# Attention with 16 heads: maxima taken in units of 512 scores, one unit in eight through ScalarE and a difference of keys, and four banks for the scores

## The chip, the cores and the metric

The kernel runs on one core of a Trainium2 chip. The metric is device time in microseconds (us) of the whole program, lower is better. PE is TensorE, DVE is VectorE, ACT is ScalarE, POOL is GpSimd and SP is SyncE.

## The reference

Four layers follow each other on x of shape (2, 2048, 256): an attention over 44 fixed offsets, eight grouped feed-forward products, a full attention with rotary positions, and the feed-forward products again. The change touches the third:

```
q, k, v = qkv[:, :, 0], qkv[:, :, 1], qkv[:, :, 2]        # 16 heads of 16
q = q * cos + rotate_half(q) * sin
k = k * cos + rotate_half(k) * sin
scores = jnp.einsum('bqhd,bkhd->bhqk', q, k) * DH ** -0.5
attn = jax.nn.softmax(scores, axis=-1)                    # over all 2048 keys
out = jnp.einsum('bhqk,bkhd->bqhd', attn, v).reshape(b, l, d)
return out @ Wo
```

The softmax subtracts the maximum over the 2048 keys of each query.

## The kernel before

The program has three stages with a barrier between them. The **local stage** works through eight chunks of 512 tokens: the first attention, the folded feed-forward weights, and at a chunk's end the rotated queries and keys of the full attention, split in two fp16 parts (`qparts`) and written to HBM (`q_d`, `k_d`). What each engine does next there is set by lists of positions (`DVE_STEPS`, `ACT_STEPS` and so on): each step has a place inside a chunk's slots, and `order_of` sorts them. The step `rotate` makes rotated values in `rope_q` (i of 0 and 1 are queries, 2 and 3 keys), ACT casts them to the high half, `rest` makes the low half on DVE, and `last` stores both.

The **attention stage** has 32 iterations (two batches, four groups of four heads, four chunks of 512 queries). An iteration y handles 16 key tiles of 128 keys. For each key tile PE computes four score matmuls, one per head, `ps_s[128 keys, 512 queries]`, ACT takes the exponential of each bank (L1422) into `pr`, and PE multiplies `pr` by the values into `ps_o` two key tiles later (`weigh`, L1353, two parts of 256 queries; each fp32 matmul shows as two). Scores are in fp16, with their contraction of 50 rows in one half of the PE array, so that two scores (heads of even and odd index) can run beside each other. Two of the 50 rows carry the negative maximum of each query, so that the exponential needs no other bias.

These maxima are computed one iteration ahead, beside the scores. For each pair of heads, each tile of 128 queries and each quarter of 512 keys, `max_unit` issues two matmuls of 48 rows (one head in each half of the array, L1311) into `ps_m[:, u % 2]`, two banks of 512 each, and DVE reduces 1024 numbers to two maxima (L1433). That is 32 units per iteration and two per key tile. After the last unit of an iteration's maxima, DVE makes the negative maxima in three small steps (L309, L311, L312), put between its next units. PE transposes them into a score bank (`max_rows`, L1318), DVE copies them out (L1447), and SP writes them into the rows of `qs` by DMA.

PE's order of work is written out in `iteration`: per key tile a max unit, two scores, the first part of `weigh`, a max unit, two scores, the second part. So a key tile has two like halves, and PE starts a half by waiting for a max bank. Scores rotate through `SB` = 3 banks: score n needs that the exponential of n-3 is done (`bank_free`). Max units rotate through two double banks. At `OUTPUT_AT` (n = 6) of the next iteration ACT copies the finished `ps_o` (L1413), which PE waits for ahead of that iteration's first `weigh`.

PSUM has eight banks: three for scores, four for maxima, one for the output.

Of the kernel before, what the change touches and what calls it, by code (L numbers as in the profile page):

```python
# [77 lines left out]
for _m, (_c, _bank, _r, _g) in enumerate(PRODUCTS):  # L78
# [64 lines left out]
    (68.079, "last", 3)]  # L143
# [17 lines left out]
    (66.977, "rest", 2), (71.781, "rest", 3)]  # L161
# [158 lines left out]
def local_stage(nc, I, D, A):  # L320

    with ExitStack() as ctx:  # L322
# [28 lines left out]
        qparts = sb("qparts", [P, 2, PARTS, CH], F16)  # L351
        nrm = sb("nrm", [P, 2], F32)
# [45 lines left out]
        def ahead_place(u):  # L398
# [21 lines left out]
            sem(n) for n in ("qkb_ps", "qkb_read", "rope_sum", "rope_high", "qparts_ready"))  # L420
        nrm_sb, nrm_ps, bound_sb, factor_step, scaled = (
# [11 lines left out]
        def parts(j, i):  # L433
            return (qparts_last if j == NG - 1 and i >= 2 else qparts)[:, i % 2]

# [12 lines left out]
        def _(sp):  # L448
# [101 lines left out]
            for s in range(2):  # L550
                sp.wait_ge(qparts_stored[s], 32 * NG)
            sp.wait_ge(nmt_stored, 64)
# [258 lines left out]
        def _(act):  # L811
# [17 lines left out]
            def step(j, what, i):  # L829
# [65 lines left out]
                elif what == "rotate":  # L895
                    act.wait_ge(rope_sum, j * 4 + i + 1)
                    act.copy(parts(j, i)[:, 0, :], rope_q[:, i % 2, :]).then_inc(rope_high, 1)
# [18 lines left out]
        def _(dve):  # L916
# [13 lines left out]
            def step(j, what, i):  # L930
# [111 lines left out]
                elif what == "rotate":  # L1042
# [12 lines left out]
                    dve.tensor_tensor(rope_q[:, i % 2, :], rope_a[:, :], rope_b[:, :],  # L1055
                                      ALU.add if i % 2 else ALU.subtract).then_inc(rope_sum, 1)
                elif what == "rest":
                    dve.wait_ge(rope_high, j * 4 + i + 1)
                    dve.tensor_tensor(parts(j, i)[:, 1, :], rope_q[:, i % 2, :], parts(j, i)[:, 0, :],
                                      ALU.subtract).then_inc(qparts_ready, 1)  # L1060

# [101 lines left out]
def full_attention(nc, I, D, A, F):  # L1163
# [4 lines left out]
    MAXU = MAXIMA * NCH  # L1168
# [4 lines left out]
    ROWS_KT = KT - AHEAD + 2  # L1173
    ROWS_AT = GRP * ROWS_KT + 2
    SCORES = KT * GRP
    OPS = SCORES + 1
    SB = 3
# [3 lines left out]
    QK_LOADS = 16 * 6 * (1 + NCH)  # L1181
    NEG = 16 * 2

    with ExitStack() as ctx:
# [4 lines left out]
        ps_m = ctx.enter_context(nc.psum_tensor("ps_m", [P, 2, 2, CH], F32))  # L1189
        ps_o = ctx.enter_context(nc.psum_tensor("ps_o", [P, CH], F32))  # L1190
        vg = sb("vg", [P, KT, GRP, SLOT], F32)
        pr = sb("pr", [P, PR_RING, GRP, CH], F32)
        q0_ld = sem("c_q0_ld")
        (qk_ld, qk_ready, va_ld, vb_ld, vc_ld, s_ps, p_ready, pv_done, m_ps, m_read, nm_step,
         nmt_ps, nmt_sb, neg_ld) = (sem("c_" + n) for n in (
             "qk_ld", "qk_ready", "va_ld", "vb_ld", "vc_ld", "s_ps", "p_ready", "pv_done", "m_ps",
             "m_read", "nm_step", "nmt_ps", "nmt_sb", "neg_ld"))
# [3 lines left out]
        def unit_place(u):  # L1201

            return u // (TILES * NCH), u // NCH % TILES, u % NCH
# [15 lines left out]
        def _(sp):  # L1219
            for n in range(2, NCH):  # L1220
# [82 lines left out]
        def _(pe):  # L1303
            def max_unit(u, taken, q, slot):

                if taken - FIRST >= 2:
                    pe.wait_ge(m_read, taken - FIRST - 1)
# [422 lines left out]
```

## Time and profile before

| | us |
|---|---|
| median of 3 runs | 2123.95 (2120.16 to 2124.56) |
| the profiled execution | 2122.61 |
| its span, first to last instruction | 2120.8 |
| local stage, up to the barrier | about 832 |
| attention stage | about 832 to 2011 |
| last stage | about 2011 to 2120.8 |

Over the span PE is busy 2011.0 us, DVE 1838.1, ACT 1523.0 and POOL 764.6. Times of one instruction (mean ns) include its tail: the next instruction of the same engine starts before it ends, so the pace of an engine is read from start to start. PE's ends are modelled. The granted clock of PE is 0.964 of full speed over the span, and full between 1000 and 1900 us.

### The profile page before, as it was taken

The page shows a single profiled execution, that of the slowest core. Times are in us where ns is not written, and L with a number is a line of the kernel's source. Part 1 is how long each engine was busy: PE and PEld are TensorE (multiplying, and loading weights), DVE is VectorE, ACT ScalarE, POOL GpSimd, SP SyncE. Part 2 cuts the span into 40 slices and gives each one's busy share as a digit, 9 for nine tenths or more (in the row PEclk, how much of TensorE's full clock was granted, in tenths as well). Part 3 has the DMA queues.
Part 4 walks back from the last instruction along what each step waited for, and adds up shares of the span by engine and source line. Part 5 has one row for each costly group of instructions (what it writes and reads, how often), then busy time and mean ns, then how long its engine had stood idle before and what let it go on. Part 6 is the DMA issues. An engine that isn't in the chain of part 4 may idle for free. (4 is left out here: it accounts for less than half of the span.)

```text
span 2120.8 us, 46870 instructions
## 1 busy us (share of the span) xinstructions
PE 2011.0 (95%) x18498; PEld 798.8 (38%) x18498; DVE 1838.1 (87%) x2195; ACT 1523.0 (72%) x3579; POOL 764.6 (36%) x1019
## 2 busy tenths in 40 slices
PE   7889999999998886999999999999999999999978
PEld 5444455555553432333333333333333333333333
DVE  3697888898886775999999999999999999999255
ACT  0155676666663413999999999999999999999911
POOL 2499899999998203603003003002000000052100
PEclk9999999999999757999999999999999999999989
DMA  8365565566567414302002001001000000031321
GB/s 279 125 140 124 127 153 136 143 158 157 127 149 161 114 34 102 81 7 55 5 7 54 7 15 46 4 25 36 5 27 5 7 24 7 9 121 58 98 71 53
DMA packets 228811, 161.86 MB, mean 76 GB/s; under 512 B 152809, under 2 KB 199865, under 8 KB 228585
## 3 DMA queue, kind: packets, MB, share of 16 engines
q1 hardware_dynamic: 198272, 112.61, 21.5%
q0 software_dynamic: 14944, 31.33, 5.5%
q10 hardware_dynamic: 15376, 14.93, 2.1%
q8 instruction: 147, 2.41, 0.5%
q14 instruction: 72, 0.58, 0.1%
HBM read 97.64 MB, written 44.11 MB: 67 GB/s over the span
## 5 line engine op out<-in xcount | busy, mean ns | idle before, releaser
L1422 ACT ACTIVATE pr<-ps_s 128x512 f32<-128x512 f32 x2048 | 1087.1, 596 | 72.7 <-PE ps_s L1335 25.9
L1433 DVE TENSOR_REDUCE mx<-ps_m 128x2 f32<-128x1024 f32 x980 | 1124.3, 1213 | 10.6 <-PE ps_m L1311 8.9
L1353 PE MATMUL ps_o<-pr,vg 128*32 128x256 f32 x8192 | 654.8, 392 | 8.1 <-ACT f_ou L1413 8.1
L588 POOL TENSOR_TENSOR room<-qs 128x512 f32<-128x512 f32 x336 | 414.8, 1268 | 79.7 <-ACT qs L855 54.4
L1335 PE MATMUL ps_s<-qs,ks 50*128 50x512 f16 x2048 | 423.2, 382 | 0.5 <-ACT pr L1422 0.5
L1311 PE MATMUL ps_m<-ks,qs 48*128 48x512 f16 x1960 | 384.5, 388 | 9.4 <-PEq L322 9.4
L1267 POOL DMA_DIRECT2D vg<-vb_d x24 | 19.6, 819 | 976.3 <-PE ps_o L1353 893.9
L1353 PEld LDWEIGHTS ps_o<-pr,vg 128*32 128x32 f32 x8192 | 162.6, 108 | 273.6 <-issue 245.6
L1311 PEld LDWEIGHTS ps_m<-ks,qs 48*128 48x128 f16 x1960 | 93.9, 92 | 413.0 <-issue 278.1
L927 DVE TENSOR_TENSOR room<-PSa,qs 128x512 f32<-128x512 f32 x368 | 234.1, 678 | 14.1 <-PE PSa L681 13.6
L1335 PEld LDWEIGHTS ps_s<-qs,ks 50*128 50x128 f16 x2048 | 188.8, 94 | 119.9 <-ACT pr L1422 38.6
L681 PE MATMUL PSa<-room,sj 128*32 128x512 f32 x1408 | 197.9, 608 | 9.1 <-POOL room L588 4.4
L878 ACT ACTIVATE attn<-PSa,red 128x44 f32<-128x44 f32 x416 | 117.0, 312 | 9.3 <-DVE red L1009 4.5
L878 ACT ACTIVATION_READ_ACCUMULATOR attn<-PSa,red 128x1 f32 x416 | 92.6, 223 | 0.0
L885 ACT COPY room<-PSa 128x512 f32<-128x512 f32 x128 | 69.2, 595 | 31.8 <-PE PSa L753 31.3
L1260 POOL DMA_DIRECT2D qs<-q_d x168 | 83.6, 504 | 1.1 <-issue 1.1
L644 PE MATMUL PSa<-tail_room 128*128 128x256 f32 x256 | 64.7, 410 | 13.7 <-DMA tail_room<-in_W2T 9.2
L890 ACT COPY oT<-PSa 128x128 f32<-128x128 f32 x64 | 17.9, 280 | 80.9 <-PE PSa L768 80.8
L603 POOL TENSOR_TENSOR far<-far,fart 128x128 f32<-128x128 f32 x128 | 69.2, 541 | 10.0
L753 PE MATMUL PSa<-ident,room 128*128 128x128 f32 x512 | 72.5, 287 | 0.3 <-DMA room<-skew 0.3
L753 PEld LDWEIGHTS PSa<-ident,room 128*128 128x128 f32 x512 | 59.9, 147 | 31.6 <-issue 28.4
L957 DVE TENSOR_REDUCE mx<-PSa 128x1 f32<-128x512 f32 x88 | 54.9, 683 | 16.3 <-PE PSa L665 16.3
(162 smaller groups left out, 1906.9 us busy)
## 6 DMA issues: line engine op xcount, KB each, us to landing
room<-skew SPq DMA_DIRECT2D x128, 208.0 KB, 4.0
skew<-attn SPq DMA_DIRECT2D x64, 164.0 KB, 4.2
tail_room<-in_W SPq DMA_DIRECT2D x32, 256.0 KB, 3.4
tail_room<-in_W2T SPq DMA_DIRECT2D x32, 256.0 KB, 4.1
vb_d<-vb SPq DMA_DIRECT2D x8, 1024.0 KB, 6.0
qs<-ks SPq DMA_DIRECT2D x26, 256.0 KB, 5.7
ks<-k_d POOLq DMA_DIRECT2D x48, 128.0 KB, 3.2
qs<-q_d POOLq DMA_DIRECT2D x180, 32.0 KB, 2.9
```

The lines of the kernel that those rows point to most:

```text
L588: pool.tensor_tensor(prod_p[:, n % RING, :], qT[:, c, :], kT[:, c, col:col + CH], ALU.mult).then_inc(prod_p_ready, 1)
L603: pool.tensor_tensor(total, total, part, ALU.add).then_inc(far_step, 1)
L681: pe.matmul(PS[SLOT * g:SLOT * (g + 1), SC_BANK, :], sj[:, BANK_J * bank + 4 * g + r, :], rhs[:, n % RING, :], start=(r == 0), stop=(r == ...
L753: tr = pe.transpose(PS[:, TURN_BANK[half], h * P:(h + 1) * P], own[:, w % 2, 4 * half + h, :], ident[:, :])
L878: ex = act.activation(attn[:, w % 2, h, :], logits[:, h, :], ACT.Exp, bias=red[:, w % 2, 0, h:h + 1], accum_out=red[:, w % 2, 1, h:h + 1])
L927: dve.tensor_tensor(prod_d[:, n % RING, :], PS[:, Q_BANK[c], :], kT[:, c, col:col + CH], ALU.mult).then_inc(prod_d_ready, 1)
L1260: pool.dma_start(qs[rows, g * NCH + n, :, :], D["q_d"][Q_STACK[i], :, heads, b * T + (1 + n) * CH:b * T + (2 + n) * CH]).then_inc(qk_ld, 16)
L1311: mm = pe.matmul(ps_m[:, u % 2, t, :], qs[rows, q, pair, tile * P:(tile + 1) * P], ks[rows, slot, pair, quarter * CH:(quarter + 1) * CH], ...
L1335: pe.matmul(ps_s[:, op % SB, :], ks[rows, slot, j // 2, kt * P:(kt + 1) * P], qs[rows, q, j // 2, :], start=True, stop=True).then_inc(s_ps, 1)
L1353: mm = pe.matmul(ps_o[SLOT * j:SLOT * (j + 1), cols], vg[:, kt, j, :], pr[:, kt % PR_RING, j, cols], start=(kt == 0 and part == 0), stop=( ...
L1422: act.activation(pr[:, kt % PR_RING, j, :], ps_s[:, place_of(y, n) % SB, :], ACT.Exp, scale=exp_scale).then_inc(p_ready, 1)
L1433: dve.tensor_reduce(mx[:, x % MX_RING, :, pair * TILES + tile, quarter], ps_m[:, u % 2, :, :], AX_X, ALU.max).then_inc(m_read, 1)
```

## The change

A max unit is now one matmul of 512 scores in one bank (two units where there was one, 64 per iteration), and `ps_m` has three banks. The freed bank goes to the scores (`SB` = 4). PE's order puts the four units of a key tile singly between the scores and the parts of `weigh`.

Of each eight units in a row, unit 1 (`is_less`) multiplies the queries by a difference of keys, the first quarter minus the second, for the odd head of a pair: ACT takes relu of it into `over` in SBUF. Unit 5 (`is_both`) is the same query tile and head with the second quarter: DVE adds `over` to it and takes the maximum, since max(a, b) = relu(a - b) + b. So DVE handles seven units of eight. The place in `mx` of the quarter left out is set to the lowest fp32 number once.

The differences are made in the local stage, twice (once per batch, in its second chunk): the rotated keys of a batch's first chunk stay in `first_k`, DVE subtracts (`diff`), ACT casts, DVE makes the low half (`diff_rest`), ACT stores to `kd_d` (`diff_last`). The attention stage loads them into `kd` beside the keys.

```diff
-    MAXU = MAXIMA * NCH
+    MAXU = 2 * MAXIMA * NCH
+    CYCLE, LESS, BOTH = 2 * NCH, 1, 5
+    QUARTERS = (0, 2, 1, 3)
+    START = FIRST + CYCLE
+    M_BANKS = 3
-    SB = 3
+    SB = 4
-    QK_LOADS = 16 * 6 * (1 + NCH)
+    QK_LOADS = 16 * (6 * (1 + NCH) + 3)
...
+            def max_unit(n, q, slot):
+                old = n - M_BANKS
+                if old >= FIRST:
+                    if is_less(old):
+                        pe.wait_ge(m_over, overs(old + 1))
+                    else:
+                        pe.wait_ge(m_read, reads(old + 1))
+                t, pair, tile, quarter = unit_place(n)
+                rows = half(t, 0, KROWS)
+                keys = kd[rows, slot, pair, :] if is_less(n) else ks[rows, slot, pair, quarter * CH:(quarter + 1) * CH]
+                pe.matmul(ps_m[:, n % M_BANKS, :], qs[rows, q, pair, tile * P:(tile + 1) * P], keys,
+                          start=True, stop=True).then_inc(m_ps, 1)
...
+                    if x == 1 and kt == (START - FIRST) // PER_TILE:
+                        pe.wait_ge(kd_ld, 16 * len(K_STACK))
+                    score(x, GRP * kt, q, slot)
                     tile_max(x, PER_TILE * kt)
-                    score(x, GRP * kt, q, slot)
                     score(x, GRP * kt + 1, q, slot)
...
                     tile_max(x, PER_TILE * kt + 1)
                     score(x, GRP * kt + 2, q, slot)
                     score(x, GRP * kt + 3, q, slot)
+                    tile_max(x, PER_TILE * kt + 2)
                     if older >= 0:
                         weigh(older // KT, older % KT, 1)
+                    tile_max(x, PER_TILE * kt + 3)
...
+            def take_less(n):
+                k = overs(n)
+                if k >= 2:
+                    dve_unit = n - 2 * CYCLE + BOTH - LESS
+                    act.wait_ge(m_read, reads(dve_unit + 1))
+                act.wait_ge(m_ps, n - FIRST + 1)
+                act.activation(over[:, k % 2, :], ps_m[:, n % M_BANKS, :], ACT.Relu).then_inc(m_over, 1)
...
+                        unit = (y + 1) * MAXU + CARRY + n - 1
+                        if is_less(unit) and unit < ITERS * MAXU:
+                            take_less(unit)
                         act.wait_ge(s_ps, y * SCORES + n + 1)
...
+                if is_both(n):
+                    dve.wait_ge(m_over, overs(n))
+                    above = over[:, (overs(n) - 1) % 2, :]
+                    dve.tensor_tensor_reduce(out=above, in0=ps_m[:, n % M_BANKS, :], in1=above, scale=1.0, scalar=LOWEST,
+                                             op0=ALU.add, op1=ALU.max, accum_out=best).then_inc(m_read, 1)
+                else:
+                    dve.tensor_reduce(best, ps_m[:, n % M_BANKS, :], AX_X, ALU.max).then_inc(m_read, 1)
...
+                elif what == "diff" and j % NCH == 1:
+                    dve.wait_ge(qparts_ready, j * 4 + i + 1)
+                    dve.tensor_tensor(rope_q[:, i % 2, :], first_k[:, i % 2, :], rope_q[:, i % 2, :],
+                                      ALU.subtract).then_inc(diff_ready, 1)
```

The order on PE in the attention stage, before. L1311 is a matmul for the maxima, L1335 a score, L1353 a part of `weigh`; the rows cover one key tile and a half.

```order
L1311 MATMUL ps_m<-ks,qs 128x512 x2
L1335 MATMUL ps_s<-qs,ks 128x512 x2
L1353 MATMUL ps_o<-pr,vg 32x256 x4
L1311 MATMUL ps_m<-ks,qs 128x512 x2
L1335 MATMUL ps_s<-qs,ks 128x512 x2
L1353 MATMUL ps_o<-pr,vg 32x256 x4
```

The same engine and stage now, one key tile (the first of two, the one with the difference `kd`): L1373 is a max unit, L1396 a score, L1414 a part of `weigh`.

```order
L1396 MATMUL ps_s<-qs,ks 128x512
L1373 MATMUL ps_m<-ks,qs 128x512
L1396 MATMUL ps_s<-qs,ks 128x512
L1414 MATMUL ps_o<-pr,vg 32x256 x4
L1373 MATMUL ps_m<-kd,qs 128x512
L1396 MATMUL ps_s<-qs,ks 128x512 x2
L1373 MATMUL ps_m<-ks,qs 128x512
L1414 MATMUL ps_o<-pr,vg 32x256 x4
L1373 MATMUL ps_m<-ks,qs 128x512
```

The two matmuls that stood together are apart: one comes between two scores or after two scores, the other directly behind a part of `weigh`.

DVE in the attention stage, at the place where an iteration's maxima end, before (with what each waits for):

```order
L309 TENSOR_REDUCE nm<-mx 128x16 [waits c_m_read]
L1433 TENSOR_REDUCE mx<-ps_m 128x2 [waits c_m_ps]
L311 TENSOR_SCALAR nmp<-nm 128x2x8 [waits c_nm_step,c_m_read]
L1433 TENSOR_REDUCE mx<-ps_m 128x2 [waits c_m_ps]
L312 SCALAR_TENSOR_TENSOR nmp<-nm,nmp 128x2x8 [waits c_nm_step,c_m_read]
```

The same place now. The two rows L1512 are one `tensor_tensor_reduce`: the add and maximum, and an instruction that writes the one result.

```order
L309 TENSOR_REDUCE nm<-mx 128x16 [waits c_mx_low,c_m_read]
L1515 TENSOR_REDUCE mx<-ps_m 128x1 [waits c_m_ps]
L311 TENSOR_SCALAR nmp<-nm 128x2x8 [waits c_nm_step,c_mx_low,c_m_read]
L1515 TENSOR_REDUCE mx<-ps_m 128x1 [waits c_m_ps] x2
L312 SCALAR_TENSOR_TENSOR nmp<-nm,nmp 128x2x8 [waits c_nm_step,c_mx_low,c_m_read]
L1512 ISA over,mx<-ps_m,over 128x512 [waits c_m_over,c_m_ps]
L1512 ISA mx 128x1
L1515 TENSOR_REDUCE mx<-ps_m 128x1 [waits c_m_ps] x3
```

The three small steps keep their spacing in scores, two units of 512 for one of 1024, and every eighth unit is missing from DVE's list.

On ACT the stage has one more instruction for eight exponentials (L1498):

```order
L1486 ACTIVATE over<-ps_m 128x512
L1498 ACTIVATE pr<-ps_s 128x512 x8
L1486 ACTIVATE over<-ps_m 128x512
L1498 ACTIVATE pr<-ps_s 128x512 x8
L1486 ACTIVATE over<-ps_m 128x512
```

Before, nothing but exponentials and one copy per iteration stood there.

## Rows read from the trace of the kernel before

**Rows 1.** Windows: stretch, PE, PEld, DVE, ACT, POOL busy (instructions), PEclk, DMA, GB/s

```profile
227.00:304.00 77.00, 76.98 (x695) 39.62 (x694) 67.43 (x101) 50.00 (x185) 70.35 (x81) 1.00 0.62 147
1000.00:1900.00 900.00, 892.92 (x9409) 282.12 (x9408) 898.71 (x883) 843.17 (x1589) 90.18 (x162) 1.00 0.09 24
```

**Rows 2.** Groups of instructions, 1000 to 1900 us: DVE

```profile
L1433 DVE TENSOR_REDUCE mx<-ps_m 128x2 f32<-128x1024 f32 x783 | 898.2, 1213 | 1.3
```

**Rows 3.** Timeline, PE alone: start us, us, instructions

```profile
1215.97 0.39 PE L1311 MATMUL ps_m<-ks,qs 48*128 48x512 f16 x2
1216.19 0.41 PE L1335 MATMUL ps_s<-qs,ks 50*128 50x512 f16 x2
1216.53 0.64 PE L1353 MATMUL ps_o<-pr,vg 128*32 128x256 f32 x8
1217.11 0.39 PE L1311 MATMUL ps_m<-ks,qs 48*128 48x512 f16 x2
1217.33 0.38 PE L1335 MATMUL ps_s<-qs,ks 50*128 50x512 f16 x2
...
1218.21 0.39 PE L1311 MATMUL ps_m<-ks,qs 48*128 48x512 f16 x2
...
1226.09 0.39 PE L1311 MATMUL ps_m<-ks,qs 48*128 48x512 f16 x2
```

**Rows 4.** Waits, 1000 to 1900 us: us in total, times, longest

```profile
PEld ps_m L1311 <- DVE mx L1433: 110.8, 269, 0.4
```

**Rows 5.** Timeline, DVE alone

```profile
1227.78 0.21 DVE L309 TENSOR_REDUCE nm<-mx 128x16 f32<-128x64 f32 x1
1227.90 1.22 DVE L1433 TENSOR_REDUCE mx<-ps_m 128x2 f32<-128x1024 f32 x1
1229.03 0.17 DVE L311 TENSOR_SCALAR nmp<-nm 128x16 f16<-128x16 f32 x1
1229.10 1.22 DVE L1433 TENSOR_REDUCE mx<-ps_m 128x2 f32<-128x1024 f32 x1
```

**Rows 6.** Timeline, ACT alone, in four short stretches

```profile
1207.85 0.58 ACT L1413 COPY f_ou<-ps_o 128x512 f32<-128x512 f32 x1
...
1244.69 0.58 ACT L1413 COPY f_ou<-ps_o 128x512 f32<-128x512 f32 x1
...
1980.99 1.09 ACT L1422 ACTIVATE pr<-ps_s 128x512 f32<-128x512 f32 x2
...
1981.94 0.63 ACT L1422 ACTIVATE pr<-ps_s 128x512 f32<-128x512 f32 x1
```

**Rows 7.** Timeline, PE and one of DVE, around the output copy and the transposed maxima

```profile
1207.71 0.39 PE L1311 MATMUL ps_m<-ks,qs 48*128 48x512 f16 x2
...
1209.15 0.39 PE L1311 MATMUL ps_m<-ks,qs 48*128 48x512 f16 x2
...
1209.58 1.23 DVE L1433 TENSOR_REDUCE mx<-ps_m 128x2 f32<-128x1024 f32 x1
...
1230.59 0.39 PE L1311 MATMUL ps_m<-ks,qs 48*128 48x512 f16 x2
...
1231.96 0.39 PE L1311 MATMUL ps_m<-ks,qs 48*128 48x512 f16 x2
```

**Rows 8.** Timeline of the local stage: units of 512 with three banks; two-input operations

```profile
783.26 2.48 DVE L957 TENSOR_REDUCE mx<-PSa 128x1 f32<-128x512 f32 x4 [0.46 <-PE PSa L665]
785.80 0.10 PEld L665 LDWEIGHTS PSa<-ks,qs 48*128 48x128 f16 x1 [0.50 <-DVE mx L957]
...
223.52 1.41 DVE L1039 SCALAR_TENSOR_TENSOR tail_room<-PSa,bcc,tail_room 128x512 f32<-128x512 f32 x2 [1.55 <-PE PSa L686]
```

**Rows 9.** The same operations by tile and line: duration ns min/median/max

```profile
L957 DVE TENSOR_REDUCE mx<-PSa x88: 629/681/693, 704.1 to 804.5; 128x1 f32<-128x512 f32 x88
L1039 DVE SCALAR_TENSOR_TENSOR tail_room<-PSa,bcc,tail_room x16: 741/748/752, 223.5 to 797.8; 128x512 f32<-128x512 f32 x16
```

**Rows 10.** Timeline, PE alone, last iteration, which computes no maxima

```profile
1996.74 0.48 PE L1335 MATMUL ps_s<-qs,ks 50*128 50x512 f16 x2
...
1998.77 0.48 PE L1335 MATMUL ps_s<-qs,ks 50*128 50x512 f16 x2
```

More of the change, by code:

```diff
@@ L434, in parts, with rotated @@
             return (qparts_last if j == NG - 1 and i >= 2 else qparts)[:, i % 2]
+        def rotated(j, i):
+            return (first_k if j % NCH == 0 and i >= 2 else rope_q)[:, i % 2, :]
         def qk_banks(j, i):
@@ L1219, in _ @@
         def _(sp):
+            load_differences(sp, 0, kd_ld)
             for n in range(2, NCH):
@@ L1303, in _ @@
         def _(pe):
-            def max_unit(u, taken, q, slot):
-                if taken - FIRST >= 2:
-                    pe.wait_ge(m_read, taken - FIRST - 1)
-                pair, tile, quarter = unit_place(u)
-                for t in range(2):
-                    rows = half(t, 0, KROWS)
-                    mm = pe.matmul(ps_m[:, u % 2, t, :], qs[rows, q, pair, tile * P:(tile + 1) * P],
-                                   ks[rows, slot, pair, quarter * CH:(quarter + 1) * CH], start=True, stop=True)
-                mm.then_inc(m_ps, 1)
+            def max_unit(n, q, slot):
[10 more added lines that the diff above has]
+                          start=True, stop=True).then_inc(m_ps, 1)
             def max_rows(x, bank):
@@ L1447, in max_rows @@
                 dve.tensor_copy(nmt[:, :], ps_s[0:PARTS * 16, bank, 0:P // 2].bitcast(F16)).then_inc(nmt_sb, 1)
+            plain = (START - MAXU) // CYCLE
+            for ring, first in ((0, 0), (1, plain), (2, 0)):
+                lower(ring, first, MAXIMA)
             for x in range(1, ITERS):
                 for e in range(MAXU):
-                    u = CARRY + e
-                    if x + u // MAXU < ITERS:
-                        max_unit(x + u // MAXU, u % MAXU)
-                    if 0 <= u - MAXU < NM_STEPS:
-                        max_parts(x, u - MAXU)
+                    n = x * MAXU + CARRY + e
+                    if n < ITERS * MAXU and not is_less(n):
+                        max_unit(n)
+                    part = (CARRY + e - MAXU) // 2
+                    if CARRY + e >= MAXU and e % 2 == 0 and part < NM_STEPS:
+                        max_parts(x, part)
+                        if x == 1 and part == NM_STEPS - 1:
+                            lower(1, 0, plain)
                     if e == PER_TILE * ROWS_KT:
```

78 lines of the change are left out of this document (58 added, 20 removed).

## The prediction

> **What bounds the kernel now.** I read the windows by stage first, then the groups of the attention stage, then short stretches of the timeline on one engine at a time. In the attention stage three engines look full: of 900 us PE is busy 893, DVE 899, ACT 843 [rows 1]. DVE's group explains its share at once: 783 reductions of 1024 scores with 1.3 us of idle time [rows 2], one start every 1.13 us (1227.90 to 1229.03, [rows 5]). One iteration takes 36.84 us (output copy to output copy, 1207.85 to 1244.69, [rows 6]; it repeats 29 times to the hundredth). DVE's own sum is 32 x 1.131 = 36.2, and the small steps add about 0.4 to 0.6.
>
> But DVE is not alone at that level. PE's timeline shows its own period: eight half key tiles from 1217.11 to 1226.09 are 8.98 us, so 2.246 us per key tile, and 16 x 2.246 = 35.94 [rows 3]. Two places per iteration are longer. The half that holds the wait for the output copy takes 1.44 instead of 1.11, and the half with the transposed maxima 1.37 instead of 1.11 [rows 7], so +0.33 and +0.27. The rest, 36.84 - 35.94 - 0.60 = 0.30, comes in the half behind each, where scores wait for one of three banks. So the PE sum is 36.84, and DVE, which falls back a little in each half, catches up at those two places. The wait list puts 110.8 us of PE's weight loads down to DVE, but in 269 pieces of 0.4 us, the length of the idle time between two groups of loads in any half [rows 4]: it is not lost time. A change that relieves DVE alone can't give back its whole relief; PE's pace of 2.246 is close behind.
>
> Inside a half the pieces are: 0.22 from the max pair to the score pair, 0.31 to 0.34 to `weigh`, 0.57 to the next max pair [rows 3]. The long halves are 0.03 longer than the short ones: there the second score starts late (the pair lasts 0.41 against 0.38), because it waits for the exponential three scores back. Short half: (2.246 - 0.03) / 2 = 1.109.
>
> **PE after the change.** The matmul count is the same. The order puts unit u7 and score s0 beside each other (opposite halves of the array), then u0 and s1, then `weigh`; then u1 and s2, s3 and u2, `weigh`, u3. So every unit still finds a partner, and I cost the reordering at nothing. With four score banks the 0.03 goes and so does the 0.30 behind the two long places. PE alone: 32 x 1.109 = 35.49, + 0.33 + 0.27 = 36.09 per iteration. That is the floor.
>
> **ACT.** When it has work, exponentials start every 0.477 us (1980.99 to 1981.94 are two, [rows 6]); one of the three there also waits for a second semaphore and costs nothing extra. 64 exponentials, 8 relus and the copy are 73 x 0.477 = 34.8 per iteration, 96% of the floor. In a cycle of two key tiles ACT is behind for four exponentials after a relu and just caught up at the end of the cycle. I count 0, with cover of 1.3 us per iteration; without it, ACT's wait would show as scores late by the difference.
>
> **DVE.** A reduction of 512 starts 0.60 us after the last (four from 783.26 end at 785.74; less 0.68 for the last, over 3, [rows 8, 9]); read more finely 0.598. Seven of eight units: per cycle of two key tiles 6 x 0.598 plus the fused one. I write the fused one as 0.598 + x. The trace does not show it. It is two instructions. From below: no faster than a reduction of the same length, and its second instruction like the smallest DVE steps, 0.07 from start to start (1229.03 to 1229.10, [rows 5]): x = 0.07. From above: the first instruction like the two-input one of L1039, which reads PSUM and SBUF and is followed by its like after 1.41 - 0.75 = 0.66 to 0.67 [rows 8, 9], the second 0.17, L311's whole duration [rows 5], because it has to wait for the first to end: x = 0.07 + 0.17 = 0.24. Between them, the nearest row (L1039 and then a small step) says 0.14, the plain reduction and a small step 0.07; I take x = 0.12.
>
> The Vector Engine (DVE) Microarchitecture Reference of the Trainium skill (section 7, Points that are easy to get wrong) says that this family of two-input instructions runs at half throughput when both sources are fp32 in SBUF. Here one source is PSUM, and the row of L1039 with one PSUM source shows full throughput, so I leave it to a rival.
>
> DVE's load is then 8 x (7 x 0.598 + x) + 0.4 + 0.1 = 34.9 per iteration, below PE. **But three single banks are a tighter ring than two double ones.** Before, two units of 1.13 us stood in the ring; now three of 0.6. Follow the ring in one cycle: DVE sits idle after u1 is left out, and starts u3 0.43 us after its matmul (1209.15 to 1209.58, [rows 7]). Then it runs u3, u4, u5, u6, u7 without a gap: u7 starts 4 x 0.598 + x = 2.39 + x later and ends 0.68 after that [rows 9]. PE's load of weights for u2 of the next cycle follows that end by 0.05 (785.80 behind 785.74, [rows 8]), and PE reaches its u3 0.88 us later (s3 and u2 together, 0.31 to `weigh`, 0.57 to u3). The ring closes with 0.43 + 2.39 + x + 0.68 + 0.05 + 0.88 = 4.44 + x. PE alone needs 4 x 1.109 = 4.436. So a cycle takes 4.44 + x: **each hundredth of x is paid eight times per iteration**, though DVE is idle 0.25 us per cycle. Queued behind the waiting load of u2 are `weigh` part 1, u3 and the next scores, so it is PE's time in full.
>
> Two of the eight cycles are those with the 0.33 and 0.27, which fall ahead of u2 and cover x there. The small step L312 now stands in the ring's gapless run (after u4): +0.08. L309, L311 and the copy of the rows fall in the idle 0.25. Iteration after: 36.09 + 0.08 + 6x = 36.17 + 6x. Against 36.84 the point of no gain is x = 0.11. With x = 0.12: 36.89, +0.05.
>
> **The sum.** 29 full iterations x 0.05 = +1.5. The last iteration and the end of the one before have no maxima: they take 2.03 us per key tile (1996.74 to 1998.77, [rows 10]) through three banks; with four they can go at ACT's 4 x 0.477 = 1.91, 0.12 x 20 key tiles = -2.4. Local stage: per batch 4 DVE instructions of 0.6, 2 casts and 2 DMA issues on ACT's queue, ahead of the next chunk's copies. PE is full there (76.98 of 77) and DVE is not (67.4) [rows 1], so 4.8 us of DVE work hide mostly; I take +1, at most +5. At the attention's start SP issues three loads of differences ahead of the query loads, and PE wants them in the third key tile: 0 to +1, counted in the 1. Sum: +0.1. The profiled execution took 2122.6 against a median of 2124.0 (+1.3), so I predict 2124 us.
>
> **Rivals.**
> A. The ring is not tight: PE's load for u2 finds its bank free, because the fused operation hides its second instruction or u7 starts earlier than I count. Then 36.17 to 36.6 per iteration, -0.67 to -0.24: 29 times that, less 1.4, is -21 to -8, 2103 to 2116. For it: DVE's load is 5% under PE's, and x near its lower bound gives the same (0.07: 36.59). Against: the ring closes within a hundredth of PE's own period, so nothing is spare.
> B. Slower: the fused operation is the one late thing, its place is the bank that u2 needs, and it decides from x = 0.13 on. With x = 0.24: 37.61, +0.77 x 29 = +22, less 1.4: 2145. For it: a result that is read out of the engine after the last element can hardly overlap the pass that makes it. Against: the small steps between reductions do overlap, 0.07.
> C. ACT becomes the bound: if relus and exponentials with two waits cost 0.1 each instead of nothing (24 per iteration), ACT needs 34.8 + 2.4 = 37.2, +0.4 x 29, so 2134. The two-wait exponential in [rows 6] speaks against it.
> D. The fused operation streams at half rate: x = 0.6, iteration 39.8, +3 x 29 = +85, 2210. By the skill's rule only where both sources are in SBUF.
>
> **How the numbers follow.** The forecast (x of 0.08 to 0.16, own range 2117 to 2131) has 0.48, A 0.23, B 0.22, C 0.04, D 0.03. A measurement can tell about 0.2% (4.2 us) from no change. Of the forecast's 0.48 about 0.13 fall below 2119.7, 0.27 within and 0.08 above 2128.2. Faster 0.13 + 0.23 = 0.36, same 0.27 + 0.03 from the near end of B = 0.30, slower 0.08 + 0.19 + 0.04 + 0.03 = 0.34. The range that holds 8 in 10 reaches into A and B: 2105 to 2142.
>
> **What would show it.** In the trace after: output copies 36.9 us apart (36.2: A; 37.3 and more: B or C). PE's long halves 1.14 gone. DVE idle about 0.25 us once per cycle, ahead of u3, and nowhere else; from the start of the fused instruction to that of the next reduction 0.72. PE's load for u2 waiting for DVE by about x, in six of eight cycles. ACT idle over 1 us per iteration. The last iteration at 1.91 per key tile. Wrong would be the whole line of thought if PE waited for DVE at other units than u2, if PE's half without waits were longer than 1.11 in the new order (a unit without a partner), or if ACT had no idle time.

## The result and the profile after

| | before | changed kernel |
|---|---|---|
| median of 20 runs each | 2124.26 us (2114.76 to 2137.77) | 2115.64 us (2108.85 to 2123.59) |
| ratio | | 0.9964, 95% interval 0.9948 to 0.9981 |
| span of the profiled execution | 2120.8 | 2112.9 |
| first matmul for the maxima in the attention stage, called its start below | 831.9 | 846.9 |
| from there to the last output copy | 1178.9 | 1156.8 |
| last stage | 110.0 | 109.2 |

The change made the kernel faster by 0.36%, 8 us. The prediction said no change, 2124 us. (On another chip the ratio was 0.9986 and its interval held 1, experiment 10.) The small difference is a sum of two large ones: in these two executions the attention stage gained 22.1 us, and the local stage ahead of it, where the differences of the keys are made, lost 15.1. (The changed kernel puts a score 0.4 us ahead of its first maximum, so counted from the stage's first matmul they are 21.7 and 14.7.) How firm the 15.1 is, a table behind the experiments tells. One execution below, the profiled one of the kernel with both moves, ran 1.5% long at a lower granted clock (0.918 against 0.965 to 0.968) and is left out of its ratio.

**The attention stage.** The windows view of the same stretch as in [rows 1] (PE, PEld, DVE, ACT, POOL busy, then PEclk, DMA and GB/s):

```profile
1000.00:1900.00 900.00, 893.55 (x9581) 265.64 (x9585) 865.84 (x1693) 896.33 (x1818) 107.23 (x195) 1.00 0.10 26
```

DVE fell from 899 to 866 and ACT rose from 843 to 896. PE's busy time hardly changed, but it got more instructions into the stretch. The groups of that stretch (busy us, mean ns of one, then the idle time before them), against [rows 2]:

```profile
L1498 ACT ACTIVATE pr<-ps_s 128x512 f32<-128x512 f32 x1594 | 812.6, 668 | 0.0
L1515 DVE TENSOR_REDUCE mx<-ps_m 128x1 f32<-128x512 f32 x1195 | 756.8, 683 | 34.2 <-PE ps_m L1373 30.9
L1512 DVE CUSTOM_DVE_ANT_0 over<-ps_m,over 128x512 f32<-128x512 f32 x199 | 135.6, 681 | 0.0
L1486 ACT ACTIVATE over<-ps_m 128x512 f32<-128x512 f32 x199 | 126.7, 637 | 3.7 <-DVE mx L1515 0.4
L1512 DVE DVE_READ_ACCUMULATOR2_ANT mx<- 128x1 f32 x199 | 16.5, 83 | 0.0
```

DVE has 34.2 us of idle time ahead of its plain reductions, where it had 1.3. The fused operation lasts as long as a plain reduction (681 against 683 ns). Its second instruction lasts 83 ns. What that one costs, only the order of starts tells. The timeline of DVE, one cycle of two key tiles (start, duration):

```profile
1206.86 0.68 DVE L1512 CUSTOM_DVE_ANT_0 over<-ps_m,over 128x512 f32<-128x512 f32 x1
1207.47 0.08 DVE L1512 DVE_READ_ACCUMULATOR2_ANT mx<- 128x1 f32 x1
1207.47 2.48 DVE L1515 TENSOR_REDUCE mx<-ps_m 128x1 f32<-128x512 f32 x4
1210.12 1.29 DVE L1515 TENSOR_REDUCE mx<-ps_m 128x1 f32<-128x512 f32 x2 [0.17 <-PE ps_m L1373]
1211.33 0.68 DVE L1512 CUSTOM_DVE_ANT_0 over<-ps_m,over 128x512 f32<-128x512 f32 x1
```

The next reduction starts 0.61 us after the fused operation, at the same 1207.47 as the read of the accumulator. Read more finely it is 0.606, so x = 0.606 - 0.598 = 0.008. The only idle time of the cycle is the one ahead of u3 (1210.12), as forecast. PE's timeline, the unit that reads the difference `kd` (u1), in two cycles:

```profile
1204.12 0.39 PE L1373 MATMUL ps_m<-kd,qs 48*128 48x512 f16 x1
...
1205.23 0.39 PE L1373 MATMUL ps_m<-ks,qs 48*128 48x512 f16 x1
...
1208.56 0.39 PE L1373 MATMUL ps_m<-kd,qs 48*128 48x512 f16 x1
...
1209.69 0.39 PE L1373 MATMUL ps_m<-ks,qs 48*128 48x512 f16 x1
...
1213.02 0.39 PE L1373 MATMUL ps_m<-kd,qs 48*128 48x512 f16 x1
```

The first cycle is 4.44 us, PE's own pace of 4 x 1.109; it is one of the two that follow a longer place. The second is 4.46: its first half, which holds u1 and u2, takes 1.13 (1208.56 to 1209.69) instead of 1.11. There PE's load of weights for u2 comes 0.05 behind the end of u7, whose bank it needs (timelines of DVE and PEld):

```profile
1208.07 0.68 DVE L1515 TENSOR_REDUCE mx<-ps_m 128x1 f32<-128x512 f32 x1
...
1208.80 0.09 PEld L1373 LDWEIGHTS ps_m<-ks,qs 48*128 48x128 f16 x1
```

So the ring of three banks is closed in the changed kernel. Read more finely, the 32 halves of one iteration are 24 of 1.109, six of 1.138 (those with u1 and u2 in six of the eight cycles), one of 1.436 with the wait for the output copy and one of 1.295 with the transposed maxima. A cycle that holds one of the six and no longer place takes 4.465. The copies of the output, which end an iteration, on ACT's timeline, with the relu beside the exponentials:

```profile
1204.61 0.60 ACT L1486 ACTIVATE over<-ps_m 128x512 f32<-128x512 f32 x1
1205.10 4.02 ACT L1498 ACTIVATE pr<-ps_s 128x512 f32<-128x512 f32 x8
1209.04 0.60 ACT L1486 ACTIVATE over<-ps_m 128x512 f32<-128x512 f32 x1
...
1216.51 0.59 ACT L1478 COPY f_ou<-ps_o 128x512 f32<-128x512 f32 x1
...
1252.68 0.59 ACT L1478 COPY f_ou<-ps_o 128x512 f32<-128x512 f32 x1
```

1252.68 - 1216.51 = 36.17, where [rows 6] had 36.84. (22 of the 29 full iterations take 36.17, the others 36.22 to 36.39.) The copies at the end lie at 1940.16, 1973.81 and 2003.75: 33.66 and 29.94 for the two iterations with few or no maxima (35.38 and 30.76 before).

**The local stage.** The stretch of [rows 1] from 227 to 304 is as before; the next chunk but one, the first that makes differences, is not (same columns):

```profile
227.00:304.00 77.00, 76.96 (x698) 39.62 (x694) 67.36 (x102) 50.45 (x184) 70.35 (x82) 1.00 0.64 148
321.00:412.00 91.00, 83.50 (x708) 42.69 (x708) 72.85 (x109) 53.24 (x190) 74.24 (x85) 0.94 0.54 126
```

The second row is the whole third chunk: the stores of x that end the chunks lie at 321.2 and 411.6, 90.4 us apart (77.0 before). PE stands for 7.5 us in two pieces. The first, on DVE's and PE's timelines (in brackets the idle time and who ended it):

```profile
366.80 3.25 DVE L1081 TENSOR_TENSOR tail_room<-first_k,tail_room 128x512 f32<-128x512 f32 x2
...
372.06 0.94 DVE L288 RECIPROCAL t_rs<-t_sd 128x128 f32<-128x128 f32 x1
```

```profile
373.05 1.55 PE L293 MATMUL PSa<-t_rs,spread 128*128 128x128 f32 x8 [2.51 <-DVE t_rs L288]
...
389.29 1.19 PE L264 MATMUL PSa<-t_xm,ones 128*128 128x512 f32 x1 [4.99 <-DVE t_xm L260]
```

The two new subtractions (L1081, step `diff`) took 3.25 us ahead of an inverse that PE waits for. The second piece is the wait of `diff_rest` (L1085) for ACT's cast:

```profile
385.58 1.05 DVE L1085 TENSOR_TENSOR first_k<-tail_room,first_k 128x512 f16<-128x512 f32 x1 [6.89 <-ACT first_k L909]
386.55 1.40 DVE L1055 SCALAR_TENSOR_TENSOR tail_room<-PSa,bcc,tail_room 128x512 f32<-128x512 f32 x2
387.87 0.68 DVE L1085 TENSOR_TENSOR first_k<-tail_room,first_k 128x512 f16<-128x512 f32 x1
388.47 0.68 DVE L260 TENSOR_TENSOR t_xm<-tail_room 128x512 f32<-128x512 f32 x1
```

DVE stood 6.89 us with the update of the residual (L1055) and the norm's input (L260) queued behind, and PE waits for the latter. The granted clock (PEclk, the third number from the end) fell to half twice, as the windows show:

```profile
373.00:377.00 4.00, 3.95 (x27) 2.37 (x31) 2.36 (x4) 0.00 (x0) 2.60 (x3) 0.58 1.05 307
377.00:387.00 10.00, 7.30 (x70) 3.34 (x62) 3.11 (x6) 6.56 (x24) 9.08 (x11) 1.00 0.47 125
387.00:394.00 7.00, 4.71 (x14) 1.57 (x15) 4.57 (x7) 0.60 (x2) 1.27 (x2) 0.52 0.00 0
```

A mean of 0.58 over 4 us is half clock for 3.4 us, 0.52 over 7 us for 6.7. The first of these stretches lies behind the first idle piece. The second lasts from 387.3 to 394.1 by the trace's records of the clock: it begins 2 us before the second piece ends (389.29) and reaches almost 5 us beyond it.

### The profile page after: what moved, and what is told of

Its sections match the earlier page's. It is cut to its first block and busy times, and to the rows that moved or that the text cites. A ratio compares the mean times of both kernels' runs of the same rounds, so it can differ in the third digit from the quotient of the medians.

```text
span 2112.9 us, 48657 instructions
## 1 busy us (share of the span) xinstructions
PE 1989.9 (94%) x18498; PEld 770.3 (36%) x18498; DVE 1792.2 (85%) x3187; ACT 1570.7 (74%) x3827; POOL 777.9 (37%) x1040
## 5 line engine op out<-in xcount | busy, mean ns | idle before, releaser
L1498 ACT ACTIVATE pr<-ps_s 128x512 f32<-128x512 f32 x2048 | 1042.8, 676 | 1.7 <-PE ps_s L1396 1.6
L1515 DVE TENSOR_REDUCE mx<-ps_m 128x1 f32<-128x512 f32 x1472 | 932.1, 684 | 45.3 <-PE ps_m L1373 41.5
L1414 PE MATMUL ps_o<-pr,vg 128*32 128x256 f32 x8192 | 655.0, 392 | 9.3 <-ACT f_ou L1478 8.6
L1396 PE MATMUL ps_s<-qs,ks 50*128 50x512 f16 x2048 | 612.4, 384 | 9.4 <-PEq L322 9.3
L1373 PE MATMUL ps_m<-ks,qs 48*128 48x512 f16 x1716 | 544.6, 384 | 0.0
L1414 PEld LDWEIGHTS ps_o<-pr,vg 128*32 128x32 f32 x8192 | 162.5, 108 | 333.8 <-issue 210.0
L1373 PEld LDWEIGHTS ps_m<-ks,qs 48*128 48x128 f16 x1716 | 142.3, 93 | 353.3 <-issue 203.7
L1512 DVE CUSTOM_DVE_ANT_0 over<-ps_m,over 128x512 f32<-128x512 f32 x244 | 166.2, 681 | 0.7 <-PE ps_m L1373 0.7
L1486 ACT ACTIVATE over<-ps_m 128x512 f32<-128x512 f32 x244 | 155.1, 636 | 5.5 <-PE ps_m L1373 1.3
L1396 PEld LDWEIGHTS ps_s<-qs,ks 50*128 50x128 f16 x2048 | 141.8, 93 | 29.5 <-ACT pr L1498 19.0
L1373 PE MATMUL ps_m<-kd,qs 48*128 48x512 f16 x244 | 94.5, 387 | 0.0
L879 ACT ACTIVATE room<-PSa,pbias 128x512 f32<-128x512 f32 (+1 forms) x48 | 33.1, 689 | 56.4 <-PE PSa L690 56.4
```

The lines of the kernel that those rows point to most:

```text
L1373: pe.matmul(ps_m[:, n % M_BANKS, :], qs[rows, q, pair, tile * P:(tile + 1) * P], keys, start=True, stop=True).then_inc(m_ps, 1)
L1396: pe.matmul(ps_s[:, op % SB, :], ks[rows, slot, j // 2, kt * P:(kt + 1) * P], qs[rows, q, j // 2, :], start=True, stop=True).then_inc(s_ps, 1)
L1414: mm = pe.matmul(ps_o[SLOT * j:SLOT * (j + 1), cols], vg[:, kt, j, :], pr[:, kt % PR_RING, j, cols], start=(kt == 0 and part == 0), stop=( ...
L1486: act.activation(over[:, k % 2, :], ps_m[:, n % M_BANKS, :], ACT.Relu).then_inc(m_over, 1)
L1498: act.activation(pr[:, kt % PR_RING, j, :], ps_s[:, place_of(y, n) % SB, :], ACT.Exp, scale=exp_scale).then_inc(p_ready, 1)
L1512: dve.tensor_tensor_reduce(out=above, in0=ps_m[:, n % M_BANKS, :], in1=above, scale=1.0, scalar=LOWEST, op0=ALU.add, op1=ALU.max, accum_ou ...
```

## The experiments

There are 12 runs: ten altered kernels, and the changed kernel and that of experiment 1 once more. Ratios are against the kernel before on the same chip. Runs without a ratio are a single execution each, and of them the iterations count. Iterations are read from the copies of the output. Of each edit the main lines are shown.

**1. `diff_rest` later.** The low halves on DVE, and with them its wait for ACT's cast, are moved behind the steps that PE needs, and so are the stores (`diff_last`). The casts stay where they were.

```diff
-(74.8, "diff_rest", 2), (75, "diff_rest", 3)]        # DVE_STEPS
+(82, "diff_rest", 2), (82.1, "diff_rest", 3)]
-(76.8, "diff_last", 2), (77.2, "diff_last", 3)]      # ACT_STEPS
+(85, "diff_last", 2), (85.2, "diff_last", 3)]
```

> The changed kernel with the low half of the key differences (diff_rest on DVE) moved from slot 75 to slot 82 of the chunk, and its store on ACT from 77 to 85; the attention stage is as it was. Theory: the local stage of the changed kernel is 15 us longer than before (barrier at 847 instead of 832) mainly because DVE stood 6.9 us at diff_rest until ACT had cast the difference, with the chunk's next norm behind it. Then this kernel has no such wait, its attention stage starts at 835 to 840, iterations stay at 36.17, and the time is 7 to 12 us below the changed kernel: ratio to before 0.991 to 0.993. Rival: the longer local stage comes from the added work itself or from scatter between executions, not from that wait: attention starts at 844 or later, ratio 0.996.

Measured: 2106.09 us, ratio 0.9940 (0.9923 to 0.9957). That is short of the expected ratio of 0.991 to 0.993. Attention starts at 835.5 instead of 846.9, the iteration is 36.17, and no wait at L1085 is left. The 11 us between the two starts are not all the wait's: the start of one and the same local stage scatters by more than that (table below). By the time it is 0.9964 - 0.9940, about 5 us, by the third and fourth chunk together about 6. The first piece stands:

```profile
370.62 1.16 PE L293 MATMUL PSa<-t_rs,spread 128*128 128x128 f32 x8 [2.50 <-DVE t_rs L288]
```

**2. No differences.** The steps `diff`, `diff_rest` and their stores are left out; `kd` is loaded from stored keys instead, so the maxima are other numbers. The two waits for the stores go too. The attention stage does the same work.

```diff
-... (71.9, "diff", 2), (72, "diff", 3), (74.8, "diff_rest", 2), (75, "diff_rest", 3)]
+... ]
-D["kd_d"][K_STACK[i], :, g * GRP + 1:(g + 1) * GRP:2, b * CH:(b + 1) * CH]
+D["k_d"][K_STACK[i], :, g * GRP + 1:(g + 1) * GRP:2, b * T + CH:b * T + 2 * CH]
```

> The changed kernel without the steps that make the key differences: the attention stage loads the plain keys of the first quarter in their place, so the maxima are not those of the reference, all else is the same. It shows the whole price of the differences in the local stage. Theory: attention starts within 1.5 us of before (832), ratio to before 0.989 to 0.991 (22 us of the attention stage, nothing given back). Rival that local stages scatter by 10 us between executions whatever is in them: the start lies anywhere from 828 to 845 and the ratio is near the changed kernel's 0.996.

Measured: 2099.18 us, ratio 0.9903 (0.9886 to 0.9921), on the chip of experiment 1. Attention starts at 831.2 (831.9 before), iterations 36.17, and PE has no gap in the third chunk:

```profile
321.00:398.00 77.00, 77.00 (x694) 39.37 (x693) 66.82 (x102) 50.29 (x184) 71.67 (x83) 1.00 0.63 148
```

This is the attention stage's gain alone: 2118.64 - 2099.18 = 19.5 us. The loss of the local stage comes from the difference steps: by the ratios 0.9964 - 0.9903, about 13 us. It also says that experiment 1 leaves 2106.09 - 2099.18 = 6.9 us of it.

**3. One more DVE instruction behind the fused operation,** a small memset. If the bank ring is tight, it costs PE time.

```diff
 op0=ALU.add, op1=ALU.max, accum_out=best).then_inc(m_read, 1)
+dve.memset(spare[:, :], 0.0)        # spare is 128 x 128
```

> The changed kernel with one more DVE instruction (a memset of 128 numbers, some 0.2 us from start to start) directly behind each fused operation, in the run of DVE that the bank ring has no room for. Ring theory (a cycle is 4.44 + x): the cycle grows by 0.2 less some hundredths, six of eight cycles pay, iterations go from 36.17 to 37.2 or 37.4. Rival, that DVE has room of its own (it is idle 0.25 us per cycle, and 5 per cent below PE): iterations stay within 0.1 of 36.17.

Measured: 2122.76 us. DVE's timeline:

```profile
1204.90 0.68 DVE L1513 CUSTOM_DVE_ANT_0 over<-ps_m,over 128x512 f32<-128x512 f32 x1
1205.57 0.17 DVE L1515 MEMSET spare<- 128x128 f32 x1
1205.65 2.42 DVE L1517 TENSOR_REDUCE mx<-ps_m 128x1 f32<-128x512 f32 x4
1208.24 1.29 DVE L1517 TENSOR_REDUCE mx<-ps_m 128x1 f32<-128x512 f32 x2 [0.17 <-PE ps_m L1374]
1209.44 0.68 DVE L1513 CUSTOM_DVE_ANT_0 over<-ps_m,over 128x512 f32<-128x512 f32 x1
```

A cycle takes 1209.44 - 1204.90 = 4.54 while DVE still has its idle time, and the iteration rose from 36.17 to 36.63 (16 copies from 1214.7 to 1764.2). I expected 37.2 or more. From the fused operation to the next reduction it is now 0.75 (x = 0.15), but that is not what u7 is late by: the four reductions behind the memset end 2.42 after their start, where they took 2.48 above. From the start of the fused operation to their end it is 3.17, against 3.09 in the changed kernel. So the memset delays the run by 0.08, and the cycle is longer by the same 0.08 (4.54 against 4.46). Six of eight cycles pay it: 6 x 0.077 = 0.46, which is 36.63 - 36.17.

**4. The same instruction in the idle gap.**

```diff
 max_unit(n)
+if n % CYCLE == 2:
+    dve.memset(spare[:, :], 0.0)
```

> The same extra DVE instruction, but directly behind unit 2 of each cycle, where DVE is idle 0.25 us until unit 3 is there. Ring theory: the idle time takes it, iterations stay at 36.17 to 36.35. If DVE's load counted wherever it stands, they would be as long as with the instruction in the run (37.2 or more).

Measured: 2115.29 us, iterations 36.18. DVE has the same load as in experiment 3, and it costs 0.01 per iteration instead of 0.46. So it is not DVE's load that counts but its place, behind the last wait of the cycle.

**5. A long instruction at the place of experiment 3,** to fit the law at a second point.

```diff
 op0=ALU.add, op1=ALU.max, accum_out=best).then_inc(m_read, 1)
+dve.memset(spare[:, :], 0.0)        # spare is 128 x 512
```

> As e3_extra_in_run, but the extra DVE instruction is a memset of 512 numbers, so x is about 0.6 (from the start of the fused one to that of the next reduction 1.2 instead of 0.606). In e3 x was 0.15 and the cycle 4.54, which puts the ring at 4.39 + x, not 4.44 + x. Ring theory: the cycle is 4.39 + 0.6 = 5.0 us, iterations 39.5 to 40.0. Rival: only DVE's total load counts, 8 x (7 x 0.598 + 0.6) + 0.5 = 38.8 per iteration.

Measured: 2219.59 us, iterations 39.62.

```profile
1209.14 0.68 DVE L1513 CUSTOM_DVE_ANT_0 over<-ps_m,over 128x512 f32<-128x512 f32 x1
...
1209.88 0.48 DVE L1515 MEMSET spare<- 128x512 f32 x1
1210.29 2.42 DVE L1517 TENSOR_REDUCE mx<-ps_m 128x1 f32<-128x512 f32 x4
...
1214.08 0.68 DVE L1513 CUSTOM_DVE_ANT_0 over<-ps_m,over 128x512 f32<-128x512 f32 x1
```

From the start of the fused operation to the end of the four reductions it is 1210.29 + 2.42 - 1209.14 = 3.57, 0.48 more than in the changed kernel, and the cycle of 4.94 is 0.48 longer than its 4.46. At this length the ring sets all eight cycles, and PE's two longer places are covered: 8 x 4.94 and 0.08 for L312 give 39.6. DVE's load alone would have given 38.8. The 4.39 + x of the expectations rests on x read from start to start; with the delay of the run in its place, the three cycles of 4.465, 4.54 and 4.94 follow one law: 4.46 and what DVE's run has grown by.

**6. Four banks for maxima, three for scores.**

```diff
-M_BANKS = 3
+M_BANKS = 4
-SB = 4
+SB = 3
```

> The changed kernel with four banks for maxima and three for scores. The bank ring is then open for the maxima, and PE waits for exponentials again. If the fourth score bank is what pays (the 0.03 of the long halves and the 0.30 behind the two long places of an iteration), iterations are 36.7 to 36.9, about those of the kernel before (36.84). If the relief of DVE pays whatever the score banks are, they stay at 36.1 to 36.3.

Measured: 2184.83 us, iterations 38.56 (15 copies from 1235.9 to 1775.8). My expectation missed by 1.7 us per iteration.

**7. Three banks for each,** to tell the missing score bank from the added one.

```diff
-SB = 4
+SB = 3
```

> The changed kernel with three score banks and three for maxima (one bank unused), so the fourth score bank alone is undone. Same reading as with four max banks: 36.7 to 36.9 if the score bank is the gain, 36.1 to 36.3 if it is not; the difference to the run with four max banks is what the ring costs at x = 0.008, by the ring theory under 0.1.

Measured: 2179.63 us, iterations 38.56 again. So the fourth score bank is worth 38.56 - 36.17 = 2.4 us per iteration, once ACT has a relu among the exponentials. A fourth bank for maxima beside three score banks is worth nothing; beside four score banks there is no room for it. The waits, 1000 to 1900 us (us in total, times, longest):

```profile
PEld ps_m L1373 <- DVE mx L1515: 153.6, 373, 0.4
PEld ps_s L1396 <- ACT pr L1498: 82.9, 234, 0.4
```

In the changed kernel no score load (L1396) waits for ACT in this stretch; here 234 do. In six of eight cycles one half of four takes 1.41 us, since its second score waits for an exponential.

**8. No share for ACT.** All units are plain reductions of 512 on DVE; no relu, no fused operation, and no place set to the lowest number.

```diff
-return n >= START and n % CYCLE == LESS      # is_less; is_both likewise
+return False
```

> The changed kernel without ScalarE's share: all units are plain reductions on DVE (the steps that make the differences stay in the local stage, their result is unused). DVE then has 64 x 0.598 + 0.5 = 38.8 us per iteration, so iterations of 38.7 to 39.0, 2 us above before: the single units cost DVE 32 x 0.065 = 2.1 more in fixed time. If instead PE's order were the bound, iterations would stay near 36.2.

Measured: 2193.98 us, iterations 38.69, which is 64 x 0.598 + 0.4. DVE was busy 900.00 of 900 us in the attention stage. The waits of PE's loads:

```profile
PEld ps_m L1374 <- DVE mx L1516: 419.3, 1328, 0.4
```

So one unit in eight off DVE brings 2.5 us per iteration against the same kernel without the share, but 1.85 of these only buy back what the units of 512 in place of 1024 cost (36.84 to 38.69; this kernel has the fourth score bank too).

**9. Differences spread out.** Here the first piece is attacked as well: the subtractions come later and apart.

```diff
-(71.9, "diff", 2), (72, "diff", 3), (74.8, "diff_rest", 2), (75, "diff_rest", 3)]
+(73.5, "diff", 2), (75.9, "diff", 3), (81, "diff_rest", 2), (82.1, "diff_rest", 3)]
-(68.9, "diff", 2), (69, "diff", 3), (76.8, "diff_last", 2), (77.2, "diff_last", 3)]
+(75.8, "diff", 2), (75.9, "diff", 3), (84, "diff_last", 2), (85.2, "diff_last", 3)]
```

> The changed kernel with all eight diff steps placed anew: the two subtractions on DVE at slots 73.5 and 75.9 instead of 71.9 and 72 (behind the next chunk's inverse and normalise, not ahead of them), the casts on ACT at 75.8 and 75.9, the low halves at 81 and 82.1, the stores at 84 and 85.2. Theory: what was left of the price in e1_rest_late (3 to 7 us) is that the two subtractions stood ahead of the inverse that PE waits for (2.5 us idle there), so here attention starts at 830.5 to 834 and the ratio to before is 0.990 to 0.992. Rival: it is the DVE time itself (1.7 us per subtraction beside POOL), and it costs the same wherever it stands: start at 835 or later, ratio 0.993 to 0.994.

Measured: 2108.22 us, ratio 0.9921 (0.9891 to 0.9951). The third chunk is 78.1 us, with no gap on PE, but the fourth 84.9, since `diff_rest` at 81 waits for a cast that ACT now reaches late. Attention started at 842.7, not at the 830.5 to 834 that I expected. (A first order, with the second subtraction at 79 and its cast at 79.5, gave no time: in it the engines wait for each other, a deadlock.) DVE's timeline:

```profile
371.90 0.68 DVE L1081 TENSOR_TENSOR tail_room<-first_k,tail_room 128x512 f32<-128x512 f32 x1
...
397.66 0.88 DVE L1085 TENSOR_TENSOR first_k<-tail_room,first_k 128x512 f16<-128x512 f32 x1 [3.45 <-ACT first_k L909]
```

**10. The changed kernel again,** on the chip of experiment 9.

> The changed kernel as it is, on the same chip as e8b_spread. Its local stage took 847 us in the first execution, and 841 and 844 in two kernels with the same local stage. Theory of the waits: the start lies between 840 and 848 again, the ratio to before is 0.996 to 0.997, and 0.004 to 0.006 above e8b_spread. Rival, scatter: start below 838 in this execution and no clear difference between the two.

Measured: 2117.86 us (12 runs), ratio 0.9986 (0.9968 to 1.0003). The wait at L1085 was 7.3 us, and attention started at 846.2, as expected. The ratio is above the 0.996 to 0.997 that I expected: on this chip the gain is smaller and its interval holds 1. Experiment 9 is 2117.86 - 2108.22 = 9.6 us faster on the same chip.

**11 and 12. Both moves together, and experiment 1 again,** on one chip. The subtractions are moved as in experiment 9, ACT's casts stay early, and `diff_rest` is late.

```diff
-(71.9, "diff", 2), (72, "diff", 3), (74.8, "diff_rest", 2), (75, "diff_rest", 3)]
+(73.5, "diff", 2), (75.9, "diff", 3), (82, "diff_rest", 2), (82.1, "diff_rest", 3)]
-(76.8, "diff_last", 2), (77.2, "diff_last", 3)]
+(85, "diff_last", 2), (85.2, "diff_last", 3)]
```

> Two moves together: the subtractions on DVE behind the next chunk's inverse (slots 73.5 and 75.9, as in e8b_spread), and the low halves and stores late with the casts where they were on ACT (68.9 and 69, as in e1_rest_late). In e8b_spread the casts had been moved back too, and DVE waited 4.7 us for them at the low halves, in the next chunk. Theory: here neither wait is there, the third and fourth chunk take 77 to 79 us each (in e8b_spread 78.1 and 84.9, in e1_rest_late 81.2 and 79.8, in the changed kernel 90.4 and 76.2), attention starts at 831 to 836, ratio to before 0.989 to 0.992. Rival: the added DVE work costs 4 us or more wherever it stands: ratio 0.993 or above.

> The kernel of e1_rest_late again, on the chip of e12_both_moves, for a comparison of the two without the chips between them. Theory: 2 to 4 us above e12_both_moves (the subtractions ahead of the inverse), ratio to before 0.992 to 0.994, attention starts at 834 to 838.

Measured: both moves 2101.91 us (2100.63 without the long execution), ratio 0.9917 (0.9901 to 0.9934); experiment 1 again 2103.98, ratio 0.9929 (0.9916 to 0.9942), start at 833.5. The two intervals overlap, so the second move's gain of 2 to 3 us isn't shown. Both beat the changed kernel and the one before. Of the kernel with both moves only the long execution has a trace; in it no wait at L1085 is left.

**The local stage in all traces.** Eight of the executions above have the local stage of the changed kernel (its own two, and experiments 3 to 8). The third and fourth chunk together (from the second chunk's store of x to the fourth's), and the start of the attention stage:

| | third and fourth chunk | start |
|---|---|---|
| before | 154.6 | 831.9 |
| no differences (2) | 154.5 | 831.2 |
| the changed kernel's local stage, eight executions | 166.3 to 169.3 | 837.3 to 850.7 |
| `diff_rest` later (1 and its repetition) | 161.0, 162.2 | 835.5, 833.5 |
| differences spread out (9) | 163.0 | 842.7 |

The two chunks are steady: the differences cost 12 to 15 us there, of which the later `diff_rest` takes away about 6. What follows, from the fourth store to the start, lasts 350 to 361 us whatever is in the kernel (355.5 before, 356.7 without differences). So a single start can't price a step of a few us, and what the second batch's differences cost is lost in that scatter.

## Why the prediction was wrong

**What bounds the stage: right.** PE's pace (1.109 per half key tile), the two longer places and the order of the stage were as worked out, and DVE is idle only ahead of u3. The iteration of 36.17 happens to be the 36.09 + 0.08 of the prediction, by terms that differ a little: 32 x 1.109 = 35.49, 0.33 for the output copy as forecast, 0.19 instead of 0.27 + 0.08 for the transposed maxima, and 6 x 0.03 = 0.17 for the ring. The two iterations without full maxima gained 1.7 + 0.8 us against the 2.4 forecast; at the end a key tile takes 1.96, not 1.91.

**The ring: right, constant and count too.** It is closed in six of eight cycles, PE's load for u2 comes 0.05 behind the end of u7, and experiments 3 and 5 lengthen the cycle by just what they delay u7. Experiment 4 shows that the same work in the gap is free. The measured cycle is 4.465; the forecast 4.44 + x with the measured x of 0.008 gives 4.45.

**The step that failed first: "I take x = 0.12".** It measured 0.008. Both bounds, 0.07 and 0.24, were too high. I had taken from the small steps beside the reductions (L309 to L312) that a second instruction costs at least 0.07 from start to start. The read of the accumulator starts with the next reduction. In the prediction's own sum, 36.17 + 6x, this one term makes 6 x (0.12 - 0.008) = 0.67 of the 0.72 per iteration between the forecast of 36.89 and the 36.17 measured; the rest is the small differences above. Over 29 iterations the 0.72 is 21 us. The time is rival A's ("36.17 to 36.6"), and so is its first cause, that the fused operation hides its second instruction. Its name, "The ring is not tight", is not borne out: the bank for u2 is not free early, and a hundredth more of delay is paid in six cycles (experiment 3).

**The other failed term: "local stage, I take +1, at most +5".** It measured 12 to 15 us in the third and fourth chunk, about 13 by the ratios of the changed kernel and experiment 2 (on different chips), and +15.1 in the start of the profiled execution. I counted the work (4.8 us of DVE) as hidden, since PE was full and DVE was not. The loss is mainly two places: the subtractions ahead of the inverse, and the wait of `diff_rest`, which is queued ahead of the residual's update and the norm. Experiment 1 takes that wait away (about 6 us), experiment 2 all of it, and experiment 9 the first place, at the price of a wait in the next chunk. I had not asked of this edit what I asked of the ring: what is queued behind the new wait. That the total came within 8.4 us of the forecast is luck: the two misses have opposite signs, -21 and +14 us in the profiled executions.

**The fourth score bank: right sign, too small.** I counted it at the 0.03 and the 0.30, 0.8 us per iteration with all its halves. Experiments 6 and 7 say 2.4. What I left out is the relu: with one in each cycle the exponentials behind it come 0.49 later (1204.61 to 1205.10 above). In experiment 7 one score of each of six cycles waits for an exponential and makes a half of 1.41 in place of 1.14, 1.6 of the 2.4; the rest lies at the two longer places. That the relu is the cause I conclude from this, no run has the new order with three score banks and no relu.

**ACT (rival C): not the bound.** ACT's starts are 36.17 / 73 = 0.495 apart on average, against 0.477 in [rows 6], which leaves the 1.3 us per iteration that I had counted. The sign that I had named, "ACT idle over 1 us per iteration", can't be read from the busy share, which is 896 of 900: the instructions last 0.67 and overlap, so that gaps of up to 0.19 don't show.

**Rivals B and D fell.** The fused operation runs at the pace of a plain reduction. The Vector Engine (DVE) Microarchitecture Reference of the Trainium skill (section 7, Points that are easy to get wrong) states half throughput for two sources in SBUF that are not bf16. Here one of the two is in PSUM and the trace shows no halving, with its 0.606; no run here has the fused operation with both in SBUF.

## What to carry to other kernels

A wait added to an in-order queue costs what is queued behind it, even in a stage where that engine is 12% idle: list, for each new step, which step that the full engine waits for stands next behind it, and put the wait behind that one. With a ring of banks, add up the loop from wait to wait rather than the engine's load; work behind the last wait is paid each turn, and work ahead of it is free. Count a step in such a loop by how much later the loop's last step ends, not by its own time from start to start: in experiment 3 these were 0.08 and 0.15. Where the sum lands within a few hundredths of the other engine's pace, the error of one unknown step times its count is the width of the forecast. And compare one execution's stages with those of its repetitions before a few us are put down to an edit.

## What the runs showed of the hardware

- Reading out the accumulator after a two-input operation of 512 costs 0.008 us: its 83 ns lie beside the next reduction, which starts at the same time.
- A memset of 128 numbers between the fused operation and the reductions put the next reduction 0.14 later, but the run of four reductions behind it was 0.06 shorter (2.42 against 2.48), so it cost 0.08 (experiment 3).
- The same subtraction of two fp32 tiles in SBUF (L1081, 128x512) took very different times in two places. By line, with min, median and max in ns, the changed kernel and then experiment 9:

```profile
L1081 DVE TENSOR_TENSOR tail_room<-first_k,tail_room x4: 899/1238/1755, 366.8 to 688.8; 128x512 f32<-128x512 f32 x4
```

```profile
L1081 DVE TENSOR_TENSOR tail_room<-first_k,tail_room x4: 681/684/769, 371.9 to 694.1; 128x512 f32<-128x512 f32 x4
```

  In the changed kernel the two of the first batch took 1.75 and 1.57 us, those of the second 0.90 each. POOL was at work beside both kernels' subtractions of the first batch. The cause wasn't tried alone.
- The same 2.5 us without matmuls made PE's granted clock fall to half (1.2 GHz) in one execution and not in another of the same kernel. Experiment 1 and then its repetition, each behind its piece of 2.50 and 2.49 us:

```profile
370.00:375.00 5.00, 4.38 (x56) 2.90 (x57) 3.75 (x6) 0.82 (x3) 4.66 (x7) 1.00 1.06 305
```

```profile
373.00:378.00 5.00, 5.00 (x54) 3.06 (x53) 4.04 (x6) 0.50 (x3) 4.19 (x4) 0.66 0.93 231
```

  The second is half clock for 3.4 us, and its third chunk took 82.8 us against 81.2. So a stall of PE can cost more than its idle time. The piece of about 5 us came with a stretch of 6.8 us at half clock in all eight executions that have it, and the stretch began before the piece ended.
